# A two-layer post-norm decoder: f1's router moved into the padding of the shared chunks, the last norm done by tiles, and the expert blocks' rows gathered to a buffer and added by VectorE

## The reference, cut to what matters

```
x = LN(x + linear_attention(x))              # L0: 16 heads, elu + 1 feature maps, output projection
x = LN(x + vocab_experts(x, ids, ctx))       # x0: 4 experts of 256 units, each token has one, by its id
x = LN(x + golden_moe(x))                    # f0: 8 experts of 256 units, all computed, weighted per token
x = LN(x + group_attention(x))               # L1: groups of 32 tokens, half of the heads rolled by 16
x = LN(x + cross_attention(x, ctx, mask))    # x1: softmax(x ctx^T / 16) ctx, masked
x = LN(x + f1(x))

def f1(x):                                   # x is [1024, 256]
    scores = softmax(x @ gate_weight.T)      # gate_weight is [8, 256]
    w, i = top_k(scores, 2)
    combine = zeros([1024, 8]); combine[t, i] = w
    y  = sum over e of combine[:, e] * ((silu(x @ G[e].T) * (x @ U[e].T)) @ Dn[e].T)   # 176 units each
    y += (silu(x @ Gs.T) * (x @ Us.T)) @ Ds.T                                           # 352 shared units
    return y
```

## Time and profile before

| what | before |
|---|---|
| runs, us | 422.52, 424.13, 425.94; median 424.13 |
| the profiled execution, us | 422.61; its span 420.5 |
| busy share of PE, DVE, ACT, POOL | 96%, 58%, 57%, 65% |
| TensorE's mean granted clock | 0.998 of full speed |
| memory traffic over the span | 38.52 MB read, 3.44 MB written, 100 GB/s |

### The profile page before, as it was taken

One profiled execution on the slowest core, in us unless ns is written; L12 is line 12 of the kernel. 1 busy time (PEld: TensorE's weight loads), 2 busy tenths in 40 slices (PEclk: granted clock), 3 DMA queues, 4 the chain that ended last, 5 costly groups with the idle time before them and its releaser, 6 DMA issues.

```text
span 420.5 us, 9389 instructions
## 1 busy us (share of the span) xinstructions
PE 405.5 (96%) x3615; PEld 353.4 (84%) x3615; DVE 241.9 (58%) x647; ACT 238.8 (57%) x430; POOL 272.8 (65%) x251
## 2 busy tenths in 40 slices
...
GB/s 240 307 105 146 53 52 87 151 63 82 70 101 105 127 30 117 133 88 32 146 25 75 39 2 113 65 78 69 174 100 88 103 135 45 163 162 151 150 27 100
DMA packets 23239, 43.09 MB, mean 102 GB/s; under 512 B 3051, under 2 KB 10859, under 8 KB 23196
## 3 DMA queue, kind: packets, MB, share of 16 engines
...
HBM read 38.52 MB, written 3.44 MB: 100 GB/s over the span
## 4 chain that ended last, share of the span: by engine, by line
PE 77%; POOL 6%; DVE 5%; ACT 4%; issue 4%; DMA 2%; SPq 1%; POOLq 0%; DVEq 0%
PE bank L557 13%; PE bank L558 12%; PE bank L560 12%; PE bank L890 7%; PE bank L892 7%; PE bank L891 7%; PE bank L970 2%; POOL h_lo L1510 2%; POOL x_tok L1467 2%; PE bank L958 1%; PE bank L909 1%; PE bank L580 1%; POOL xs_dram L1461 1%; PE bank L744 1%; PE bank L940 1%
## 5 line engine op out<-in xcount | busy, mean ns | idle before, releaser
L1510 POOL TENSOR_TENSOR h_lo<-hraw,h_hi 128x512 fp32r<-128x512 f32 x68 | 88.3, 1312 | 56.4 <-ACT h_hi L1260 56.2
L557 PE MATMUL bank<-xT_hi,pk_hi 128*128 128x512 f32 x240 | 97.0, 404 | 1.1 <-POOL pk_lo L1516 1.1
L558 PE MATMUL bank<-xT_hi,pk_lo 128*128 128x512 f32 x240 | 94.8, 395 | 0.7 <-issue 0.7
L1260 ACT ACTIVATE h_hi<-hraw 128x512 fp32r<-128x512 f32 x68 | 42.8, 629 | 65.1 <-DVE hraw L1909 65.1
L1516 POOL TENSOR_TENSOR pk_lo<-pk_raw,pk_hi 128x512 fp32r<-128x512 f32 (+1 forms) x44 | 74.7, 1699 | 4.0 <-ACT pk_hi L1278 3.8
L560 PE MATMUL bank<-xT_lo,pk_hi 128*128 128x512 f32 x240 | 75.5, 396 | 0.0
L1909 DVE TENSOR_TENSOR hraw<-bank,sil 128x512 f32<-128x512 f32 x68 | 46.9, 690 | 48.3 <-PE bank L560 19.3
L890 PE MATMUL bank<-pk_hi,h_hi 128*128 128x256 f32 x240 | 68.9, 287 | 1.0 <-POOL h_lo L1510 0.8
L892 PE MATMUL bank<-pk_hi,h_lo 128*128 128x256 f32 x240 | 67.8, 282 | 0.0
L891 PE MATMUL bank<-pk_lo,h_hi 128*128 128x256 f32 x240 | 67.8, 282 | 0.0
L557 PEld LDWEIGHTS bank<-xT_hi,pk_hi 128*128 128x128 f32 x240 | 45.2, 188 | 11.2 <-POOL pk_lo L1516 1.5
...
## 6 DMA issues: line engine op xcount, KB each, us to landing
...
```

Of the source, the lines that this page charges most:

```text
L557: pe.matmul(o, w(kc)[0], x(kc)[0], start=kc == 0, stop=False)
L558: pe.matmul(o, w(kc)[1], x(kc)[0], start=False, stop=False)
L1260: A(h_hi[:, row, at * 512:(at + 1) * 512], hraw[:, s % 2, :], ACT.Copy).then_inc(sems["hid_hi"], 1)
L1510: pool.tensor_tensor(h_lo[:, row, q], hraw[:, s % 2, :], h_hi[:, row, q].bitcast(F32), ALU.subtract).then_inc(sems["hid_lo"], 1)
```

## The change

**Router of f1.** The 8 gate rows are put into rows 0 to 7 of the shared gate's padded chunks, and the shared rows start at row 32. `CH_S` stays 3. The gate product of unit 40 (unit 54 in half 1) so has the router's logits on its first 8 partitions, turned: expert on the partition, token on the column. DVE transposes 32 partitions of that bank in blocks of 32 (`turned_logits`), and softmax and top two run on 32 partitions (`turned_first`, `turned_second`); one block transpose writes `cwT` (`turned_weights`). PE's steps a.22 and a.24 and ACT's a.24 go; Silu of units 40 and 54 waits for the transposed logits. `save_weights` and `spread_weights` stay as they are, and so does SP's string. On DVE half 0 has a0.22 in its old place, a0.23 after e3.12, a0.27 after m41 and a0.28 after a1.5; half 1 has a1.22, a1.23, a1.27, a1.28 ahead of m54.

**Last norm.** Of half 1, tile 3 is summed alone in bank 6 and tile 2 alone in bank 5. PE does tile 2's last products (y44 to y47) and then tile 3's (z44 to z47); DVE, POOL and SP treat the two one by one, so there is one more store.

**Fetch.** The indirect transfers Q0 to Q3 write to the buffer `o_tok` and no longer add; DVE adds each tile (in x1.50 to x1.53). In POOL's string Q2 and Q3 stand behind l8 and l9. l3 and l4 move from POOL to DVE.

**Order.** On ACT, G2 comes ahead of h10, G16 inside e0.6 and e1.6, G25 ahead of h47, e2.2 ahead of s48, G30 ahead of e2.7; on POOL G16, G25 and G30 move likewise; on DVE e2.2 comes ahead of o48 and e3.2 ahead of m48. The diff, cut:

```diff
-CH_S = -(-FS // P)
+CH_S = -(-(GS + FS) // P)
...
 PE_ORDER
-... e0.7 e1.7 d18 a0.22 d19 g40 u40 g41 e2.12 u41 e3.12 g42 a0.24 a1.3 a1.4 u42 d20 a1.5 ...
+... e0.7 e1.7 d18 g40 d19 u40 g41 e2.12 u41 e3.12 g42 a1.3 a1.4 u42 d20 a1.5 ...
-... g53 u53 a1.22 d31 d32 g54 d33 u54 g55 a1.24 u55 ...
+... g53 u53 g54 d31 d32 u54 d33 g55 u55 ...
-... d43 e44 e45 e46 f44 e47 f45 f46 f47
+... d43 e44 e45 e46 y44 y45 e47 y46 y47 z44 z45 z46 z47
 ACT_ORDER
-... s10 r0.4 h10 G2 s11 ...
+... s10 r0.4 G2 h10 s11 ...
-... s38 e0.6 e1.6 h38 s39 e0.7 e1.7 D15 G16 h39 ... h40 a0.24 s41 ...
+... s38 e0.6 G16 e1.6 h38 s39 e0.7 e1.7 D15 h39 ... h40 s41 ...
-... s47 h47 D24 G25 D25 G26 D26 e2.1 e3.1 s48 e2.2 e3.2 h48 s49 ... e2.7 e3.7 h52 s53 G30 ... h54 a1.24 s55
+... s47 G25 h47 D24 D25 G26 D26 e2.1 e3.1 e2.2 s48 e3.2 h48 s49 ... G30 e2.7 e3.7 h52 s53 ... h54 s55
 POOL_ORDER
-... l2 P0 l3 P1 l4 P2 P3 l5 l6 l7 G1 D1 r0.0 r0.1 Q0 Q1 Q2 Q3 l8 l9 G2 l10 D2 ...
+... l2 P0 P1 P2 P3 l5 l6 l7 G1 D1 r0.0 r0.1 Q0 Q1 l8 l9 Q2 G2 Q3 l10 D2 ...
-... e1.5 l38 D15 l39 G16 ... l46 l47 D24 e3.0 e2.1 e3.1 G25 D25 ... l51 l52 G30 ... y0 w0 w1
+... e1.5 G16 l38 D15 l39 ... l46 G25 l47 D24 e3.0 e2.1 e3.1 D25 ... l51 G30 l52 ... y0 w0 w1 w2
 DVE_ORDER
-... m4 m5 k4 ... a0.23 m40 e2.12 e3.12 a1.3 a1.4 m41 m42 a1.5 a1.6 ...
+... m4 l3 m5 l4 k4 ... m40 e2.12 e3.12 a0.23 a1.3 a1.4 m41 a0.27 m42 a1.5 a0.28 a1.6 ...
-... e2.0 e3.0 o48 m48 e2.2 e3.2 e2.3 ... a1.22 a1.23 m54 ... w0 w1 z1
+... e2.0 e3.0 e2.2 o48 e3.2 m48 e2.3 ... a1.22 a1.23 a1.27 a1.28 m54 ... w0 w1 w2 z1
...
-        cwT = sb("cwT", [P, HT * P])
+        cwT = sb("cwT", [GS, HT * P])
+        turned = pT[0:GS, 0, 0:HT * P]
+        turned_e = turned.rearrange("p (b e) -> p b e", e=GS)[:, :, 0:E1]
+        most = sb("most", [GS, HT * NG])
+        prob, below = (bo1[0:GS, n * P:(n + 1) * P].rearrange("p (b e) -> p b e", e=E1) for n in range(2))
+        picked = sb("picked", [GS, HT * NG, E1])
...
+                    alone = u >= U_F1 + N1 and t == HT - 1
+                    o = sum_part(3) if alone else bank[4 + t // 2][:, (t % 2) * D:(t % 2 + 1) * D]
...
-                    elif t % 2 and m % N1 == N1 - 1:
+                    elif u == U_F1 + 2 * N1 - 1 and t or t % 2 and u == U_F1 + N1 - 1:
...
-                elif i == 22:
-                    route(8 + h, 1, 2 + h)
-                elif i == 24:
-                    pe.wait_ge(sems["rt_cw"], h + 1)
-                    if h == 0:
-                        wait_x(5)
-                    for t in range(HT):
-                        m = pe.transpose(bank[7][0:E1, t * P:(t + 1) * P], fb[:, T0 + t, :], ident)
-                    m.then_inc(sems["cwT_ps"], 1)
 
...
+                elif s in (S_F1, S_F1 + N1):
+                    act.wait_ge(sems["rt_lg"], 3 + (s > S_F1))
...
+            def rstd_last(j):
+
+                T = HT + j + 1
+                pool.wait_ge(sems["ln_var"], halves_before(11) + 1 + j)
+                m = pool.tensor_tensor(rstd[:, T:T + 1], var_e[:, T:T + 1], mhalf[:, 0:1], ALU.pow)
+                if j == 1:
+                    link(m)
+                    m = pool.tensor_tensor(shift[:, T:T + 1], minus_mean[:, T:T + 1], rstd[:, T:T + 1], ALU.mult)
+                m.then_inc(sems["ln_rstd"], 1)
+
...
-                pool.indirect_dma_start(x_tok[:, HT + t, :], None, ys_dram,
-                                        bass.IndirectOffsetOnAxis(ap=slot_i[:, t:t + 1], axis=0),
-                                        compute_op=ALU.add).then_inc(sems[f"x0_got{t // 2}"], 16)
+                pool.indirect_dma_start(o_tok[:, t, :], None, ys_dram,
+                                        bass.IndirectOffsetOnAxis(ap=slot_i[:, t:t + 1], axis=0)).then_inc(sems[f"x0_got{t // 2}"], 16)
 
...
+                    link(TT(x_tok[:, T, :], x_tok[:, T, :], o_tok[:, j, :], ALU.add))
...
+            def hidden_low(s):
+                u, c = unit_of(s)
+                dve.wait_ge(sems["hid_hi"], s + 1)
+                row, at = place(u, c)
+                q = slice(at * 512, (at + 1) * 512)
+                TT(h_lo[:, row, q], hraw[:, s % 2, :], h_hi[:, row, q].bitcast(F32), ALU.subtract
+                   ).then_inc(sems["hid_lo"], 1)
+
...
+            def turned_logits(h):
+
+                s = S_F1 + N1 * h
+                dve.wait_ge(sems["gate_ready"], s + 1)
+                if h:
+                    dve.wait_ge(sems["cwT_done"], 1)
+                dve.transpose(turned, gate_bank(s)[0:GS, :]).then_inc(sems["rt_lg"], 1)
+                dve.wait_ge(sems["rt_lg"], 3 + h)
+                link(dve.tensor_reduce(most[:, :], turned_e, axis=AXX, op=ALU.max))
+                TT(below, turned_e, per_turned(most[:, :]), ALU.subtract).then_inc(sems["rt_dist"], 1)
+
+            def first_of(score):
+
+                link(dve.tensor_reduce(most[:, :], score, axis=AXX, op=ALU.max))
+                link(TT(below, score, per_turned(most[:, :]), ALU.is_equal))
+                order = from_eight.unsqueeze(1).to_broadcast([GS, HT * NG, E1])
+                link(TT(below, below, order, ALU.mult))
+                link(dve.tensor_reduce(most[:, :], below, axis=AXX, op=ALU.max))
+                return order, per_turned(most[:, :])
+
+            def turned_first(h):
+
+                dve.wait_ge(sems["rt_exp1"], h + 1)
+                link(dve.tensor_reduce(most[:, :], prob, axis=AXX, op=ALU.add))
+                link(dve.reciprocal(most[:, :], most[:, :]))
+                link(TT(prob, prob, per_turned(most[:, :]), ALU.mult))
+                link(TT(picked[:, :, :], *first_of(prob), ALU.is_equal))
+
+            def turned_second():
+
+                link(STT(turned_e, picked[:, :, :], -2.0, prob, ALU.mult, ALU.add))
+                link(TT(below, *first_of(turned_e), ALU.is_equal))
+                link(TT(picked[:, :, :], picked[:, :, :], below, ALU.add))
+
+            def turned_weights(h):
+
+                link(TT(turned_e, prob, picked[:, :, :], ALU.mult))
+                if h:
+                    dve.wait_ge(sems["cw_saved"], 16)
+                dve.transpose(cwT[:, :], turned).then_inc(sems["cwT_done"], 1)
 
...
+            def last_tile(t):
+
+                T = HT + t
+                dve.wait_ge(sems["sum_ps"], t + 2)
+                TT(x_tok[:, T, :], sum_part(t), x_tok[:, T, :], ALU.add).then_inc(sems["sum_added"], 1)
+                dve.wait_ge(sems["sum_added"], t + 1)
+                link(dve.bn_stats(stats[:, t, :], x_tok[:, T, :]))
+                link(dve.bn_aggr(mv[:, T, 0:2], stats[:, t, :]))
+                moments(slice(T, T + 1))
+
+            def last_part(j):
+
+                if j:
+                    last_tile(j + 1)
+                    return
+                add_pair(1, 0).then_inc(sems["sum_added"], 1)
+                dve.wait_ge(sems["sum_added"], 2)
+                example_stats(11, 0)
 
             def last_apply():
 
                 T = 2 * HT - 1
-                dve.wait_ge(sems["ln_rstd"], halves_before(11) + 2)
-                TS(x_tok[:, T, :], x_tok[:, T, :], rstd[:, T:T + 1], shift[:, T:T + 1], ALU.mult, ALU.add
+                dve.wait_ge(sems["ln_rstd"], halves_before(11) + 3)
+                TS(x_tok[:, T, :], x_tok[:, T, :], minus_mean[:, T:T + 1], rstd[:, T:T + 1], ALU.add, ALU.mult
                    ).then_inc(sems["last_done"], 1)
 
...
+    gate[0:E1] = a["L1_ffn_gate_weight"]
+    gate[GS:GS + FS] = sgu[0:FS]
+    up[GS:GS + FS] = sgu[FS:]
+    down[GS:GS + FS] = sdn.T
...
```

More of the change, by code:

```diff
@@ L42 @@
 QH = 4
-CONST_W = P + BLK + GS + 8 + QH
+CONST_W = P + BLK + GS + 8 + QH + E1
 BZ = GS + 1
@@ L161 @@
 h18 s19 h19 G7 s20 D7 h20 s21 h21 s22 G8 h22 s23 h23 D8 G9 D9 s24 h24 s25 e0.11 e1.11 e0.12 e1.12 G10 h25 s26 h26 s27
 S1 D10 a0.4 S2 h27 s28 G11 h28 s29 h29 s30 D11 G12 a0.9 D12 G13 h30 s31 h31 s32 h32 s33 h33 D13 G14 s34 e0.1 e1.1 D14
-e0.2 e1.2 h34 s35 G15 h35 s36 e0.3 e1.3 e0.4 e1.4 h36 s37 h37 s38 e0.6 e1.6 h38 s39 e0.7 e1.7 D15 G16 h39 D16 G17 D17
-G18 a0.22 s40 D18 e2.11 e3.11 e2.12 e3.12 h40 a0.24 s41 S3 a1.4 h41 s42 h42 S4 G19 D19 G20 D20 G21 s43 h43 a1.9 s44
-D21 G22 D22 G23 D23 h44 s45 h45 s46 G24 h46 s47 h47 D24 G25 D25 G26 D26 e2.1 e3.1 s48 e2.2 e3.2 h48 s49 e2.3 e3.3 h49
```

163 lines of the change are left out of this document (75 added, 88 removed).

## The result

The changed kernel took 437.19 us (median of 6 runs, 436.44 to 438.53), the kernel before 423.27 us (6 runs, the three of the table and three more, 422.01 to 425.94): a ratio of 1.033, with a 95% interval of 1.0298 to 1.0361. Forecast were 431.0 us and a range of 426 to 434. So the sign was right, and the size was not: 13.9 us for 6.85. The profiled execution of the changed kernel took 438.53 us, with a span of 436.4; it is the longest of its six, and its span lies 15.9 us above the 420.5 of before. So 2.0 us of what the two traces differ by are not in the medians.

The account below looks back on a forecast made before the run. TensorE, busy 96% of the span, was taken as the bound. Gains of 4.35 us against losses of 11.2 (9.2 wait, 2.0 clock) gave net +6.85 on the median of 424.13: 431.0 us, range 426 to 434.

Parts of the forecast that it names:

- the queue: SP's string, half 0: later cwT save delays S4 behind it; new TensorE wait of 9.2 us before g43, bounds 8.1 and 10.5.
- h_lo: Subtractions of units 3 and 4 move from GpSimd to DVE, shortening TensorE's wait at d2: 0.4 us gained, bounds 0 and 1.1.
- the wait for l9: Two gathers behind l9 on GpSimd remove TensorE's wait at d4: 0.9 us gained, bounds 0.4 and 0.95.
- the router of half 1 off TensorE: Half 1: 16 narrow matmuls and four transposes leave a dense TensorE: 2.05 us gained, bounds 1.7 and 2.2.
- The plain gather: Fetch on GpSimd: issue taken as 1.1 us, between the scatter's 1.04 and the accumulating gather's 1.58.
- The last norm: End of kernel: two rounds of about 1.3 us follow the last matmul, not one of 2.0; 0.2 gained, bounds -0.3 and 1.2.
- DVE's four new additions lie in its idle time: Fetch: DVE's additions, 1.65 us together, fit ahead of r1.0 and cost nothing; uncovered they would cost 1.65.
- the router's work on VectorE in half 0: Half 0: a0.28 behind a1.5, narrow operations about 0.2 us each, counted only for making cwT about 12 us later.
- the same chain: Half 1, DVE's a1.22 to a1.28: some 25 operations of about 0.2 us, ending before TensorE needs m54.
- the clock: Behind g43's wait: idle TensorE falls to the low clock, slow matmuls cost 2.0 us, bounds 0 and 2.1.
- The nine matmuls of the start: TensorE's first matmuls, called ungranted: 632 ns each against 404 later; 9 x 0.228 priced the clock at 2.0 us.

## Why the prediction had the sign and missed the size

**Right: the queue.** The main step holds as it was worked out: `cwT` behind a1.5, the save, S4, G19, g43. Forecast 9.2 us, measured 9.62, and moving S4 gives 10.6 us back. `cwT` was there at 287.2 and not at 279.3, and TensorE came to g43 at 290.1 and not at 282.4. Both were late by the waits that the forecast had missed, so the wait kept its length.

**Right: what left GpSimd's and TensorE's way.** `h_lo` 0.41 us (forecast 0.4, half of a bound, so that it fits is luck), the wait for l9 0.96 (0.9), the router of half 1 off TensorE 2.29 (2.05). The plain gather issues in 0.99 us on average (forecast 1.1), a little less than the lower of its two bounds, 1.04. The last norm gave 0.53 (0.2): two rounds of one tile follow the last matmul, but the first begins 0.1 us after that matmul's start.

**Wrong: "DVE's four new additions lie in its idle time".** Priced at nothing, at 1.65 us uncovered; they cost 3.4 by the ledger, and 3.8 us come back when the gathers go first. The step took an operation's duration from a row with one operand in PSUM for one with both in SBUF, and took idle time for granted where m11, which TensorE needs, stands right behind the addition. The Trainium skill ("SBUF — State Buffer", "Who interferes with whom" and the summary of rules) has a rule against this part of the change, which the forecast missed: a VectorE instruction with two SBUF inputs contends with a GpSimd instruction that reads SBUF, and the second to issue blocks until the first has finished. The runs agree as far as one instruction goes (0.62 to 1.06 us where GpSimd ran beside it, against 0.41 with an operand in PSUM). They go beyond it behind an indirect transfer: 5.48 and 6.64 us, through four instructions. The kernel before had a row of it too: a 28-column operation at 57.47 us took 0.90 beside GpSimd's `h_lo`, and 0.18 in the changed kernel at 58.76, where GpSimd only issues a transfer:

```profile
57.47 0.90 DVE L1754 TENSOR_TENSOR pT<-pT,con 128x28 f32<-128x28 f32 x1
```

```profile
58.76 0.18 DVE L1759 TENSOR_TENSOR pT<-pT,con 128x28 f32<-128x28 f32 x1
```

**Wrong: the router's work on VectorE in half 0 had no price for TensorE.** The forecast counted only how late it makes `cwT`. But a0.23 stands ahead of a1.3, and a1.4 on TensorE waits for a1.3: 2.54 us, of which a0.23's stand beside GpSimd is the greater part (2.34 us for 0.28 in one operation). Its operations were estimated at 0.2 us and take 0.24 to 0.28 alone. Behind that wait came 1.61 us of slow matmuls. In half 1 the same chain, which the forecast had end before TensorE needs m54, holds it: a growth of 1.21 us, with a wait of TensorE of 0.73 us for `hraw` at 377.73.

**Half right: the clock.** It does fall inside the kernel, as the step said, and the price of 2.0 us stands against 1.27 in this trace, 1.4 to where the distance settles. But it is no constant. Of the six kernels here that wait ahead of g43, the three with waits of 8.65 to 9.08 us lost 4.0 to 4.3 us to the slow matmuls, the three with 9.45 to 10.32 us 1.4 to 2.2. The nine matmuls of the start gave the length of one slow matmul (632 ns; 0.63 us behind g43's wait), but not how many run slowly. The forecast called them ungranted, but the trace gives the granted clock as 1.00 there, so only their length speaks for it. The rule quoted from the Trainium skill ("TensorE: Matmul & The Clock Gate", Part 1: an idle TensorE falls back to the low clock) agrees with the windows behind g43's wait, 0.53 and 0.50 granted. What the step left out is that a shorter wait can bring the low clock too, as the one at 274.86 did.

By terms, the two that were missed make 3.4 + 2.54 + 0.35 + 1.61 = 7.9 of the 9.05 us between the ledger's 15.9 and the forecast's 6.85.
